# Degrees by row sums on VectorE in place of a TensorE product, with the instruction order written anew

## What is computed

```python
# layer 0: h = (1+eps) x + A^T x ; relu(h W1 + b1) W2 + b2 ; masked
# layer 1: degree = A.sum(-1); relu([x, (A^T x)/degree] W^T + b)
# layer 2: D^-1/2 (A + I) D^-1/2 x W + b, with D = rowsum(A + I)
# layer 3: for every edge i,j: sum_j A[i,j] * (layernorm(relu(x_i Wa + x_j Wb + b1) W2 + b2) * gamma + beta)
x = _layernorm(x + _L0_gnn_ref(x, adj, nodemask, ...))
x = _layernorm(x + _L1_gnn_ref(x, adj, adj, ...))
x = _layernorm(x + _L2_gnn_ref(x, adj, ...))
x = _layernorm(x + _L3_gnn_ref(x, adj, ...))
```

## Time and profile before

| | us |
|---|---|
| median of 3 runs | 449.63 (449.41 to 449.93) |
| profiled execution | 449.61, of which the span 447.9 |

### The profile page before, as it was taken

One profiled execution on the slowest core, in us unless ns is written; L12 is line 12 of the kernel. 1 busy time (PEld: TensorE's weight loads), 2 busy tenths in 40 slices (PEclk: granted clock), 3 DMA queues, 4 the chain that ended last, 5 costly groups with the idle time before them and its releaser, 6 DMA issues. The chain is left out here.

```text
span 447.9 us, 14059 instructions
## 1 busy us (share of the span) xinstructions
PE 429.5 (96%) x3391; PEld 403.8 (90%) x3391; DVE 422.7 (94%) x1555; ACT 393.8 (88%) x1001; POOL 353.6 (79%) x651
## 2 busy tenths in 40 slices
PE   7599989999999999999999999999999999999993
PEld 3599989999999999898999999999999999999992
DVE  6999999999999999998999999999999999999976
ACT  2378979999999899979899999999999999999994
POOL 3569979999999899953776878787878787878772
PEclk9989999999999999999999999999999999999998
DMA  6134334445444743232422223222323232323111
GB/s 225 43 86 124 101 127 159 154 157 159 155 157 152 240 162 120 80 129 78 136 89 73 88 66 92 66 92 64 94 64 94 64 94 63 95 65 97 59 37 50
DMA packets 50939, 47.60 MB, mean 106 GB/s; under 512 B 5584, under 2 KB 42576, under 8 KB 50896
## 3 DMA queue, kind: packets, MB, share of 16 engines
q1 hardware_dynamic: 49760, 46.45, 33.7%
q10 hardware_dynamic: 1136, 0.66, 0.5%
HBM read 28.22 MB, written 18.87 MB: 105 GB/s over the span
## 5 line engine op out<-in xcount | busy, mean ns | idle before, releaser
L1621 PE MATMUL bank<-w2c,hE 128*128 128x128 f32 x512 | 68.3, 277 | 0.4 <-ACT bank L928 0.4
L1621 PEld LDWEIGHTS bank<-w2c,hE 128*128 128x128 f32 x512 | 63.5, 192 | 2.6 <-issue 0.7
L1289 DVE TENSOR_TENSOR ym<-bank,wE 128x512 f32<-128x512 f32 x64 | 43.4, 684 | 4.3 <-POOL wE L775 3.3
L1264 DVE TENSOR_REDUCE ssum<-sqE 128x4 f32<-128x512 f32 x63 | 42.7, 678 | 3.0 <-ACT sqE L945 2.7
L1122 DVE BATCH_NORM_STATS2 stats<-t 128x6 f32<-128x128 f32 x192 | 44.5, 273 | 1.0 <-issue 1.0
L945 ACT ACTIVATE sqE<-bank 128x512 f32<-128x512 f32 x63 | 38.0, 603 | 8.0 <-PE bank L1621 8.0
L915 ACT ACTIVATE hE<-bank,front 128x512 f32<-128x512 f32 x64 | 43.5, 680 | 1.5 <-PE bank L1601 1.5
L742 POOL TENSOR_TENSOR half<-ym 128x512 f32<-128x512 f32 x31 | 39.6, 1276 | 5.7 <-DVE ym L1289 2.1
L775 POOL TENSOR_TENSOR wE<-erstd,fits 128x12 f32<-128x12 f32 x31 | 6.6, 213 | 44.8 <-DVE erstd L1278 44.8
L726 POOL TENSOR_TENSOR gHl<-gH,gHu 128x512 fp32r<-128x512 f32 x32 | 40.8, 1276 | 1.2 <-ACT gHu L899 1.2
L928 ACT ACTIVATE bank<-b2c 128x512 f32<-128x512 f32 x62 | 37.4, 604 | 0.5 <-DVE ym L1289 0.4
(11 more groups left out here) (192 smaller groups left out, 1643.6 us busy)
## 6 DMA issues: line engine op xcount, KB each, us to landing
hh_scratch<-hh SPq DMA_DIRECT2D x32, 256.0 KB, 2.2
gH<-hh_scratch SPq DMA_DIRECT2D x32, 256.0 KB, 2.7
A<-adj_groups SPq DMA_DIRECT2D x32, 128.0 KB, 2.1
res_scratch<-res SPq DMA_DIRECT2D x32, 128.0 KB, 2.0
gRES<-res_scratch SPq DMA_DIRECT2D x32, 128.0 KB, 2.0
AT<-adjT_groups SPq DMA_DIRECT2D x31, 128.0 KB, 2.2
out<-y SPq DMA_DIRECT2D x30, 128.0 KB, 1.8
X<-x_groups SPq DMA_DIRECT2D x29, 128.0 KB, 2.2
```

Source lines behind the costliest of these rows:

```text
L1264: nc.vector.tensor_reduce(ssum[q][:, g * ELL:(g + 1) * ELL], sqE[g][:, :, :], AX.X, ALU.add).then_inc(b[f"ssE{g}_ready"], 1)
L1289: nc.vector.tensor_tensor(ym[q][:, g, :, :], YE_ps[g], spread_last(wE[q][:, g * ELL:(g + 1) * ELL]), ALU.mult).then_inc(b[f"ymE{g}_ready"], 1)
L1621: last = nc.tensor.matmul(ps[:, i, :], hidden[:, i * P:(i + 1) * P], w2c[:, :], start=False, stop=i == tiles - 1, skip_group_check=seeded)
```

## The change

The product, its copy and the two shapes of `sums` go. VectorE sums the rows of A itself, finds the holes and counts, and makes the second norm's shift in one instruction; GpSimd multiplies beta with the degrees. The moments of all engines, and those of the edge stage and the passage, are new. `PERIOD`, `APART`, `PERIOD3` and `START3` stay.

```diff
-        sums = sb("sums", [P, SLOTS, GROUP, P + 1])
-        bdeg, deg = sums[:, :, :, 0:P], sums[:, :, :, P]
+        bdeg = sb("bdeg", [P, SLOTS, GROUP, P])
+        deg = sb("deg", [P, SLOTS, GROUP])
...
             def next_at(k, r, n):
                 if not is_last(r):
-                    sp.wait_ge(s["sums_psum"], n)
...
             def next_a(k, r, n):
                 if not is_last(r):
                     sp.wait_ge(s["xT_psum"], n)
+                    sp.wait_ge(s["deg_ready"], n)
-            dense_stages = [(24.2, next_a), (25.28, next_x), (25.66, next_at), (26.27, keep(ot, ot_s, "ot_ready", ot_stored)),
-                     (58.51, keep(res, res_s, "res_ready", stored)), (69.62, keep(hh, hh_s, "hh_ready", stored))]
+            dense_stages = [(27.17, next_a), (18.95, next_x), (30.09, next_at), (34.38, keep(ot, ot_s, "ot_ready", ot_stored)),
+                     (63.47, keep(res, res_s, "res_ready", stored)), (62.85, keep(hh, hh_s, "hh_ready", stored))]
...
-            def find_holes(k, r, n):
...
-            def keep_counts(k, r, n):
...
-            def negate_mean(k, r, n):
...
-            def make_shift(k, r, n):
...
+            def spread_degrees(k, r, n):
+
+                if isinstance(r, int) and r == 0:
+                    pool.wait_ge(s_const, 16)
+                pool.wait_ge(s["deg_ready"], n)
+                wait_past(pool, s["res_ready"], n - SLOTS)
+                nc.gpsimd.tensor_tensor(bdeg[:, k, :, :], spread_rows(C["beta"]), spread_cols(deg[:, k, :]), ALU.mult).then_inc(s["bdeg_ready"], 1)
...
-            dense_stages = [(3.9, add_scaled), (20.34, add_identity), (20.37, mark_edges), (26.78, find_holes), (28.51, keep_counts), (33.57, negate_mean),
-                     (34.21, make_shift), (34.26, guard_root), (35.9, scale_adj), (37.09, add_bias2), (48.2, residual)]
+            dense_stages = [(8.03, add_scaled), (20.78, add_identity), (18.39, mark_edges), 
+                     (35.3, guard_root), (35.94, scale_adj), (39.2, add_bias2), (40.83, spread_degrees), (61.58, residual)]
...
-            def keep_sums(k, r, n):
...
+                def ln_shift(k, r, n):
+                    dve.wait_ge(s[f"rstd{layer}"], n)
+                    wait_past(dve, s[f"x{layer + 1}_ready"], n - SLOTS)
+                    nc.vector.scalar_tensor_tensor(shift1[k][:, :], mv[layer][k][:, :, 0], -1.0, rstd[layer][k][:, :], ALU.mult, ALU.mult).then_inc(s["shift1"], 1)
...
+            def sum_rows(k, r, n):
+
+                dve.wait_ge(a_loaded[k], 16 * r + 16)
+                wait_past(dve, s["bdeg_ready"], n - SLOTS)
+                wait_past(dve, s["found_ready"], n - SLOTS)
+                nc.vector.tensor_reduce(deg[:, k, :], A[k][:, :, :], AX.X, ALU.add).then_inc(s["deg_ready"], 1)
...
+            def find_holes(k, r, n):
+
+                dve.wait_ge(s["deg_ready"], n)
+                wait_past(dve, s["dis_ready"], n - SLOTS)
+                nc.vector.tensor_scalar(hole[:, k, :], deg[:, k, :], -1.0, None, ALU.is_equal)
+                nc.vector.scalar_tensor_tensor(found[:, bass.ds(SLOTS * r + k, 1), :].rearrange("p o c -> p (o c)"), deg[:, k, :], -1.0, deg[:, k, :],
+                                               ALU.is_equal, ALU.add).then_inc(s["found_ready"], 1)
...
-            dense_stages = [(5.48, find_flaws), (14.94, sum0), (15.62, stats0), (16.57, var0), (19.4, rstd0), (20.43, apply0), (26.49, degrees), (27.21, sum1a),
-                     (28.48, sum1b), (30.57, stats1), (31.6, inverse_root), (31.93, var1), (32.89, rstd1), (39.51, sum2),
-                     (41.27, stats2), (42.85, var2), (44.78, rstd2)]
+            dense_stages = [(12.63, find_flaws), (14.72, sum0), (15.93, stats0), (16.39, var0), (17.26, rstd0), (20.02, apply0), (22.68, sum_rows), (25.48, degrees), (23.22, find_holes), (27.31, sum1a),
+                     (28.24, sum1b), (29.1, stats1), (30.86, inverse_root), (29.39, var1), (32.79, rstd1), (33.44, make_shift), (40.04, sum2),
+                     (40.14, stats2), (41.25, var2), (43.74, rstd2)]
...
-            def count_row(k, r, n):
-
-                wait_past(pe, s["sums_ready"], n - 1)
-                pe.wait_ge(at_loaded[k], 16 * r + 16)
-                for g in range(GROUP):
-                    last = nc.tensor.matmul(sums_ps[:, g, :], AT[k][:, g, :], beta1[:, :], start=True, stop=True)
-                last.then_inc(s["sums_psum"], 1)
...
-            dense_stages = [(5.87, hidden0), (7.19, mlp0a), (12.19, mlp0b), (21.57, count_row), (22.18, turn1), (24.73, project1), (36.61, aggregate2),
-                     (38.48, project2), (49.49, turn3), (54.26, project3)]
+            dense_stages = [(6.17, hidden0), (10.25, mlp0a), (13.06, mlp0b), (20.82, turn1), (23.17, project1), (35.95, aggregate2),
+                     (38.08, project2), (49.38, turn3), (51.3, project3)]
```

More of the change, by code:

```diff
@@ L278, in gnn_stack @@
         at_loaded = [sem(f"at_loaded{k}") for k in K4]
-        names = ["a0_ready", "ai_done", "ad_ready", "sums_psum", "sums_ready", "hole_found", "found_ready", "rdeg_ready", "rsq_ready", "dis0_done", "dis_ready",
+        names = ["a0_ready", "ai_done", "ad_ready", "deg_ready", "bdeg_ready", "found_ready", "rdeg_ready", "rsq_ready", "dis0_done", "dis_ready",
                  "ot_ready", "unlike_done", "hT_psum", "hT_ready", "u_psum", "rT_ready", "y_psum",
@@ L681, in mark_edges @@
                 nc.gpsimd.tensor_tensor(ot[k][:, :, :], AT[k][:, :, :], spread_rows(ident[:, :]), ALU.subtract).then_inc(s["ot_ready"], 1)
-            def find_holes(k, r, n):
-                pool.wait_ge(s_setp, 3)
-                pool.wait_ge(s["sums_ready"], n)
-                nc.gpsimd.tensor_scalar(hole[:, k, :], deg[:, k, :], -1.0, None, ALU.is_equal).then_inc(s["hole_found"], 1)
-            def keep_counts(k, r, n):
-                pool.wait_ge(s["hole_found"], n)
-                nc.gpsimd.tensor_tensor(found[:, bass.ds(SLOTS * r + k, 1), :].rearrange("p o c -> p (o c)"), deg[:, k, :], hole[:, k, :], ALU.add).then_inc(s["found_ready"], 1)
             def guard_root(k, r, n):
@@ L851, in root_rowsum @@
                 nc.scalar.activation(rsq[:, k, :], found[:, bass.ds(SLOTS * r + k, 1), :].rearrange("p o c -> p (o c)"), ACT.Sqrt, bias=ones_f[:, 0:1]).then_inc(s["rsq_ready"], 1)
-            def keep_sums(k, r, n):
-                wait_past(act, s["res_ready"], n - SLOTS)
-                wait_past(act, s["found_ready"], n - SLOTS)
-                wait_past(act, s["rdeg_ready"], n - SLOTS)
-                act.wait_ge(s["sums_psum"], n)
-                nc.scalar.activation(sums[:, k, :, :], sums_ps, ACT.Copy).then_inc(s["sums_ready"], 1)
             def apply1(k, r, n):
@@ L994, in apply_out @@
                     act.dma_start(out_d[u * GROUP:(u + 1) * GROUP, :, :].rearrange("g p f -> p g f"), y4[q][:, :, :]).then_inc(out_stored[q], 16)
-            dense_stages = [(6.13, keep_hT), (9.59, relu_u), (18.14, ln_std(0)), (22.88, keep_xT), (25.51, keep_sums), (26.81, keep_p), (29.16, root_rowsum),
-                     (32.43, ln_std(1)), (34.71, apply1), (37.63, keep_gT), (44.5, ln_std(2)), (46.32, apply2), (51.26, keep_x3T),
-                     (54.46, keep_hh)]
+            dense_stages = [(8.32, keep_hT), (10.58, relu_u), (16.92, ln_std(0)), (21.66, keep_xT), (26.44, keep_p), (27.22, root_rowsum),
+                     (32.26, ln_std(1)), (33.83, apply1), (37.06, keep_gT), (41.81, ln_std(2)), (45.58, apply2), (50.84, keep_x3T),
+                     (53.73, keep_hh)]
             edge_stages = [("spu", split_upper), ("kS", keep_S), ("kST", keep_ST), ("r0", hidden_ell(0)),
@@ L1115, in _ @@
             dve.wait_ge(s_const, 16)
-            nc.vector.tensor_copy(beta1[:, 0:P], C["beta"])
             def layer_norm(layer):
@@ L1158, in sum0 @@
                 last.then_inc(s["t0_done"], 1)
+            def sum_rows(k, r, n):
[3 more added lines that the diff above has]
+                nc.vector.tensor_reduce(deg[:, k, :], A[k][:, :, :], AX.X, ALU.add).then_inc(s["deg_ready"], 1)
             def degrees(k, r, n):
-                dve.wait_ge(s["sums_ready"], n)
+                dve.wait_ge(s["deg_ready"], n)
                 wait_past(dve, s["z_done"], n - SLOTS)
                 nc.vector.reciprocal(rdeg[:, k, :], deg[:, k, :]).then_inc(s["rdeg_ready"], 1)
+            def find_holes(k, r, n):
+                dve.wait_ge(s["deg_ready"], n)
+                wait_past(dve, s["dis_ready"], n - SLOTS)
+                nc.vector.tensor_scalar(hole[:, k, :], deg[:, k, :], -1.0, None, ALU.is_equal)
+                nc.vector.scalar_tensor_tensor(found[:, bass.ds(SLOTS * r + k, 1), :].rearrange("p o c -> p (o c)"), deg[:, k, :], -1.0, deg[:, k, :],
+                                               ALU.is_equal, ALU.add).then_inc(s["found_ready"], 1)
             def inverse_root(k, r, n):
@@ L1193, in sum2 @@
                 last.then_inc(s["t2_done"], 1)
-            stats0, var0, rstd0, apply0 = layer_norm(0)
```

(8 more changed lines are left out.)

65 lines of the change are left out of this document (26 added, 39 removed), and 85 rows, old and new, of tables (FIRST, T3).

## The result

The changed kernel takes 461.8 us (median of 4 runs, 461.19 to 461.97) against 449.7, a ratio of 1.0267 with a 95% interval of 1.0249 to 1.0285. The profiled execution has 461.19 us, span 459.5. Forecast were 463.1 us and a range of 449 to 477.

The account below looks back on a forecast made before the run. Dense stage bound by PE at 5.53 us a group, VectorE with GpSimd close at 5.15; afterwards VectorE at 5.94. 7.0 us gained by PE, 20.5 lost on VectorE: 449.6 + 13.5 = 463.1 us, range 449 to 477.

Parts of the forecast that it names:

- PE's relief: Dense stage: PE loses count_row, 0.44 us a group, round 5.53 to 5.09; pace could fall to VectorE's 5.15, gaining 7.0 us.
- VectorE's work: Dense stage: four added instructions, 0.33 us for the row sum and 0.21 for three small ones, 4.58 to 5.12 us a group.
- The waits: VectorE waiting for GpSimd: find_flaws, pair L1139, make_shift, L1183 and the find_holes pair, 0.19 each times 0.86, 0.82 us a group.
- The round: VectorE's dense-stage time a group after the change, work 5.12 plus waits 0.82, 5.94 us; 20.5 us lost on VectorE.
- The sign that the prediction named for GpSimd: Gaps in GpSimd's dense-stage row, where it had none; expected about 5.1 us of work in a round of about 5.9.
- GpSimd's and ScalarE's exchange: GpSimd swaps four 128x2 instructions for one 128x256 multiplication, ScalarE loses keep_sums (386 ns), off the path: counted as nothing.
- The edge stage: Changes in order alone, units of 7.47 us with PE full: no change taken, bounds of 4 us either way.
- the second: Rival: new small VectorE instructions cost no wait, old waits stay: 5.69 us a group, +7.0, 456.6 us; chance 0.13 with neighbours.
- The first: Rival: VectorE's waits collapse as GpSimd gets room; at 0.13 us of waits the round is 5.25, 445 us; chance 0.14 faster.

Follow-up runs that it names:

- the ring open: Changed kernel with the flaw search moved on VectorE to just behind the row sum, and the row sum replaced by a constant fill: 458.39 us, ratio 1.0191.
- the link opened: Changed kernel with the flaw search moved on VectorE to between the row sum and the next statistics, work unchanged: 458.81 us, ratio 1.0208.

## Why the prediction came out, step by step

**PE's relief: right in kind, too large.** PE has gaps now, and with the product alone gone GpSimd and VectorE are late next. But the pace then is 5.30, not 5.15, and the gain 2.3 us, not 7.0: 5.15 was read from three steps right behind the split, and the step behind the split loses 2.1 us when PE has less to do.

**VectorE's work: the prices held.** The row sum costs 0.303 from start to start (forecast 0.33); the sum-and-compare 0.07; the shift 0.08 where it does not wait; the compare without its wait 0.05. (The 0.21 for three of them was a slip: 0.153 less 0.07 is 0.08 each, 0.25.) Counted over the changed kernel's usual steps, VectorE's work without waits is 5.2 us against 5.12.

**The waits: five places forecast at 0.82 us, 0.47 seen**: 0.24 at the compare, 0.2 at the flaw search, the rest at the shift. The two old places, L1183 and the pair L1139, lost theirs (0.34 and 0.23 in before's later steps); the pair now starts as GpSimd's pause ends (100.80 and 100.83), beside its small guarded root. So of the five places named, the flaw search, the pair of find_holes and the shift wait and two do not, and in find_holes it is not the instruction that was meant. The compare is the one that the forecast's sum left out, on the strength of L1221. The rule cited there, of the Trainium skill (SBUF — State Buffer, Who interferes with whom), has the fast form of tensor_scalar among those that need the shared ports; the trace agrees with it here, 374 ns where 0.13 us is the least.

**The round: 5.94 forecast, 5.63 seen.** Of the 13.5 us the usual steps brought 4.2. The forecast came near because of terms that it did not have or left out: the turns, 3.7; the step behind the split, 1.4; the last three dense steps, 3.4, taken at nothing; against them the passage, -1.6. So the sum was right within 2 us **by errors that offset each other**, and the term that failed is "5.12 + 0.82", by 0.31 us a step, 8 us in all.

**The cause: VectorE as the bound, wrong.** "VectorE's round" was to be work plus waits. The runs show that VectorE's row is full because its waiting is counted as busy: 0.24 us of its work taken away changes nothing (462.13; 458.39 with the ring open), and the pace follows the link from bdeg's end over the flaw search to GpSimd's root (0.34 us more there, 0.32 more a step; the link opened, 0.30 less). "So found_ready and dis come earlier; no one waits long for them now, and I count nothing" is the sentence that missed it: GpSimd waits 0.45 us for the inverse root in each step. This holds for the usual steps, 4.2 of the 11.6 us of span; for the other terms no run shows a cause. The sign that the prediction named for GpSimd, gaps where it had none, was there; its reason was not spare time.

**GpSimd's and ScalarE's exchange** was nothing, as forecast, by its own work: 5.0 us a step now (the seven tensors and some 0.15 for the guarded root), and 5.0 before, both from start to start. **The edge stage** moved by 0.1 us in 225; its 4 us of bounds were not used.

**The rivals.** The one nearest is the second, 5.69 us a step: its step is what was seen, its 456.6 us lack the turns and the ends. The first, in which the waits collapse when GpSimd gets room, fell: GpSimd got room, and it stood in it.

**What stays open**: why the turn of the loop costs 1.1 us here, and why the last three dense steps went from 4.2 to 5.3 us on the mean. For the turns the new order is the likely reason: with all of the new work in the old order, VectorE idles 0.75 us at most at a turn, and these steps (6.76, 6.39, 6.29) are no longer than its usual 6.7. For the last steps it is not: there they take 16.2 us, as long as in the changed kernel (15.9), and 12.6 with the row sum alone. They go with the rest of the moved work; with which part wasn't tried.

## What to carry to other kernels

An engine that shares its ports with another can show a full row and not be the bound: a wait for the ports is counted as busy, so look at the same instruction's least duration, and at whether its end falls on the end of the other engine's. Where two in-order engines wait for each other, follow the chain from one engine's last instruction round to its next start. Work on it counts in full (0.32 of 0.34 us here); work off it can be free, as the row sum was when it was taken away, or push another instruction into a wait and count after all, as it did when made twice. A pause on the chain can be what keeps a second, worse collision away. Price a moved order as a term of its own: here the same instructions took 488 us in one order and 462 in another.

## What the hardware showed unexpectedly

The clock granted to PE fell in the changed kernel behind the split of the bias, where PE waits for VectorE. Busy time by stretch, with the granted clock third from last, in the changed kernel:

```profile
63.00:65.00 2.00, 0.04 (x1) 0.00 (x0) 1.85 (x8) 0.41 (x2) 0.00 (x0) 1.00 0.39 100
65.00:67.00 2.00, 1.22 (x8) 1.19 (x9) 2.00 (x14) 1.00 (x3) 1.68 (x4) 0.92 0.00 0
67.00:69.00 2.00, 2.00 (x6) 1.34 (x6) 2.00 (x11) 1.05 (x3) 2.00 (x3) 0.50 0.54 197
69.00:71.00 2.00, 2.00 (x15) 2.00 (x14) 1.80 (x15) 1.33 (x4) 1.42 (x4) 0.72 0.41 134
```

and in the one before:

```profile
63.00:65.00 2.00, 0.48 (x5) 0.28 (x4) 1.97 (x17) 0.94 (x4) 0.64 (x2) 1.00 0.00 0
65.00:67.00 2.00, 2.00 (x16) 1.89 (x16) 2.00 (x9) 2.00 (x7) 2.00 (x6) 1.00 0.08 18
67.00:69.00 2.00, 2.00 (x21) 1.99 (x20) 2.00 (x16) 2.00 (x8) 2.00 (x4) 1.00 0.89 302
```

In the changed kernel PE is idle nearly all of 63 to 65 us and part of the next two, and then runs at the lower of its two levels, 1.2 GHz, through 67 to 69; in before it is busy again from 65 us on and keeps 2.4 GHz. The step in question is 6.48 against 5.05 us. In the runs with the product or the row sum taken away the clock of 64 to 72 us is 0.57 and 0.79, with 7.15 and 6.75 us for that step. A likely reading is that before, PE lagged behind and had work in hand when VectorE stopped for the split, and that a PE that is no longer behind pays for a pause of others twice, with the pause and with the clock. That the clock is what makes the step long was not tried by itself, and one run speaks against the clock alone: with the row sum added and PE's product kept, the clock of 64 to 72 us is 0.79 too, and the step is 5.92, only 0.24 over that run's usual 5.68.
